# Decoder block in one kernel: the attention loop's links set further apart, with a third score buffer, and the last state-space group's output taken from PSUM

## The reference

```python
scores = jnp.einsum('bsgrd,btgd->bgrst', xq, xk) / math.sqrt(HEAD_DIM) + mask
probs = jax.nn.softmax(scores, axis=-1)
out = jnp.einsum('bgrst,btgd->bsgrd', probs, xv)
x = layernorm(x + mixer(x)); x = layernorm(x + attention(x, ctx, ctx, 0, mask)); x = layernorm(x + ffn(x))
```

## Time and profile before

| | us |
|---|---|
| median of 3 runs | 1813.44 |
| the profiled execution's own time | 1810.98 |
| its span in the trace | 1809.3 |
| PE busy in the span | 1692.5 (94%) |
| DVE busy | 1204.6 (67%) |
| ACT busy | 1107.4 (61%) |
| POOL busy | 710.1 (39%) |

### The profile page before, as it was taken

One profiled execution on the slowest core, in us unless ns is written; L12 is line 12 of the kernel. 1 busy time (PEld: TensorE's weight loads), 2 busy tenths in 40 slices (PEclk: granted clock), 3 DMA queues, 4 the chain that ended last, 5 costly groups with the idle time before them and its releaser, 6 DMA issues.

```text
span 1809.3 us, 26326 instructions
## 1 busy us (share of the span) xinstructions
PE 1692.5 (94%) x9160; PEld 1285.1 (71%) x9160; DVE 1204.6 (67%) x2257; ACT 1107.4 (61%) x2352; POOL 710.1 (39%) x588
## 2 busy tenths in 40 slices
PE   5999999999999999999999999999999867668998
PEld 4777887888788878887788778777877633333556
DVE  4766677767775768577858685868586766555443
ACT  3767485748484949484949484948594545655321
POOL 3354444435452536253626362646263411112000
PEclk8999999999999999999999999999999888889999
DMA  5232222313131323132303131313132800001000
GB/s 192 82 94 90 74 92 84 111 53 106 69 111 54 123 61 115 41 123 82 119 31 122 68 134 41 123 52 124 41 123 69 158 20 1 1 1 36 7 18 24
DMA packets 76551, 138.88 MB, mean 77 GB/s; under 512 B 6786, under 2 KB 13954, under 8 KB 76164
## 3 DMA queue, kind: packets, MB, share of 16 engines
q1 hardware_dynamic: 76420, 137.21, 24.2%
HBM read 134.55 MB, written 2.63 MB: 76 GB/s over the span
## 4 chain that ended last, share of the span: by engine, by line
PE 41%; DVE 34%; ACT 18%; issue 7%; DMA 0%; DVEq 0%; POOL 0%; SPq 0%; ACTq 0%
DVE conv L727 13%; PE ps_hs L1090 6%; ACT ps_dec L528 6%; PE ps_hs L1091 6%; PE ps_hs L1092 6%; DVE xdt L751 4%; DVE m_sb L760 4%; ACT L528 3%; ACT sq_tmp L538 3%; PE ps_y L1314 3%; PE ps_hs L243 3%; DVE ps_y L768 3%; PE ps_hs L245 2%; PE ps_hs L244 2%; PE ps_hs L1275 2%
## 5 line engine op out<-in xcount | busy, mean ns | idle before, releaser
L727 DVE SCALAR_TENSOR_TENSOR conv<-ps_hs,cw,conv 128x508 f32<-128x508 f32 (+2 forms) x432 | 319.2, 739 | 36.8 <-ACT conv L492 26.6
L375 POOL TENSOR_SCALAR_AFFINE_SELECT cum_bc<-cum_bc 128x1024 f32<-128x1024 f32 x128 | 140.4, 1097 | 503.0 <-DMA cum_bc<-cum_scratch 500.9
L528 ACT ACTIVATE ps_dec<-cum_bc,neg_cum 128x128 f32<-128x128 f32 x1024 | 308.7, 356 | 0.8
L760 DVE TENSOR_TENSOR m_sb<-ps_dec,cb 128x512 f32<-128x512 f32 x256 | 169.5, 685 | 154.7 <-ACT ps_dec L528 154.7
L243 PE MATMUL ps_hs<-x_hi,w_hi 128*128 128x512 f32 x576 | 231.8, 402 | 15.8 <-DVE conv L727 8.0
L243 PE MATMUL ps_gate<-x_hi,w_hi 128*128 128x512 f32 x576 | 239.5, 416 | 0.0
L492 ACT ACTIVATE conv<-ps_hs,cbias,cw 128x512 f32<-128x512 f32 x144 | 110.5, 769 | 189.6 <-PE ps_hs L245 189.6
L245 PE MATMUL ps_gate<-x_hi,w_lo 128*128 128x512 f32 x576 | 226.3, 393 | 0.0
L244 PE MATMUL ps_hs<-x_lo,w_hi 128*128 128x512 f32 x576 | 225.4, 391 | 0.0
L245 PE MATMUL ps_hs<-x_hi,w_lo 128*128 128x512 f32 x576 | 225.3, 391 | 0.0
L244 PE MATMUL ps_gate<-x_lo,w_hi 128*128 128x512 f32 x576 | 224.2, 389 | 0.0
(11 more groups left out here) (141 smaller groups left out, 3139.3 us busy)
## 6 DMA issues: line engine op xcount, KB each, us to landing
cum_bc<-cum_scratch SPq DMA_DIRECT2D x128, 512.0 KB, 4.1
w_raw<-w_in SPq DMA_DIRECT2D x145, 256.0 KB, 4.7
wo_raw<-w_out SPq DMA_DIRECT2D x64, 256.0 KB, 5.0
g_acc<-x_t SPq DMA_DIRECT2D x4, 512.0 KB, 5.8
acc<-x_nat SPq DMA_DIRECT2D x1, 2048.0 KB, 9.7
k_rep<-ctx_t SPq DMA_DIRECT2D x8, 256.0 KB, 12.0
out<-y_out SPq DMA_DIRECT2D x8, 256.0 KB, 2.0
wg_sb<-w_gate SPq DMA_DIRECT2D x1, 1792.0 KB, 12.3
```

Of the source, the lines that this page charges most:

```text
L528: x = sc.activation(ps_dec[e][:, cols], cum_bc[bh][:, e, cols], ACT.Exp, bias=neg_cum[:, bh * HB + b, head:head + 1])
L727: v.scalar_tensor_tensor(out=dst, in0=src, scalar=cw[:, at, TAPS - 1 - n:TAPS - n], in1=dst, op0=ALU.mult, op1=ALU.add).then_inc(S["tap"], 1)
L760: v.tensor_tensor(flat(m_sb[:, q]), ps_dec[q % 2][:, :], flat(half(cb, q // 2)), ALU.mult)\
```

## The change

It touches four places; nothing before the last pass of the mixer is changed. What each chunk computes is the same.

1. **Links and buffers of attention.** PE's loop index i now does scores(i+1), values(i-4), turn_probs(i-2); DVE's does keep_turned(i-3), masked(i, 0), masked(i, 1); ACT's does keep_turned(i-3), exponentials(i-1, 0), exponentials(i-1, 1), with keep_values between them and keep_queries ahead of them. `pr`, `pr_t` and `neg_max` get a third buffer.
2. **Values.** The two products of a chunk wait together for both copies.
3. **The mixer's last pass.** `square_sums` goes ahead of the last quarter of the products. DVE adds `g_acc * rstd_g` to `acc` (first_part), and then `ps_hs * rstd_g` straight from the bank (second_part), in place of adding the bank to `g_acc` first.
4. **The drain.** turn_values for the last two halves of sequence 7, its statistics, the second norm's second half and its transposes lie beside hidden tiles 1 to 9, before 0 to 7.

```diff
+X2_STEPS = (27, 29, 31, 33)
-        neg_max = sb3("neg_max", [P, 2, 2 * REP], F32)
+        neg_max = sb3("neg_max", [P, 3, 2 * REP], F32)
-        sb3("fill_w", [P, 2664], F32)
+        pr2 = sb3("pr2", [P, 2 * REP, SEQ], F32)
+        pr_t2 = sb3("pr_t2", [P, 2, HALF], F32)
+        sb3("fill_w", [P, 752], F32)
...
@@ ACT: exponentials and keep_turned use [i % 3] @@
-                need(act, S["pv_ps"], 2 * (i - 2) + 1)
+                need(act, S["pv_ps"], 2 * (i - 3) + 2)
...
-            for i in range(CHUNKS + 2):
-                b, c = i // KD, i % KD
-                if i < CHUNKS:
-                    exponentials(i, 0)
-                if 1 <= i <= CHUNKS:
-                    keep_turned(i - 1)
-                if i < CHUNKS:
-                    exponentials(i, 1)
-                if i >= 3 and i % 2:
-                    keep_values((i - 3) // 2)
-                if c == 3 and b + 1 < BATCH:
-                    keep_queries(b + 1)
-                if i == 4 * HB + 3:
+            for i in range(1, CHUNKS + 3):
+                if 0 <= i - 3 < CHUNKS:
+                    keep_turned(i - 3)
+                if i % KD == 1 and i // KD + 1 < BATCH:
+                    keep_queries(i // KD + 1)
+                if i - 1 < CHUNKS:
+                    exponentials(i - 1, 0)
+                if i % 2 == 0 and i >= 6:
+                    keep_values((i - 6) // 2)
+                if i - 1 < CHUNKS:
+                    exponentials(i - 1, 1)
+                if i == 23:
                     root(2, 0, slice(0, HB))
-                if c == 1 and HB < b < BATCH:
-                    x2_high(b - HB - 1, BACK_PS)
-                if i == CHUNKS - 1:
-                    x2_high(HB - 1, BACK_PS)
+                if i in X2_STEPS:
+                    x2_high(X2_STEPS.index(i), BACK_PS)
...
@@ DVE: the mixer's last pass @@
-            def last_group(b):
-                add_group(GROUPS - 1, b)
-                dve.wait_ge(S["acc_ok"], BATCH * (GROUPS - 1) + b + 1)
-                row_stats(1, b)
+            def second_part(b):
+                dve.wait_ge(S["o_ps"], BATCH * (2 * GROUPS - 1) + b + 1)
+                dve.wait_ge(S["acc_ok"], BATCH * (GROUPS - 1) + b + 1)
+                v.scalar_tensor_tensor(out=acc[:, b, :], in0=ps_hs[b % 2][:, :], scalar=rstd_g[:, b:b + 1],
+                                       in1=acc[:, b, :], op0=ALU.mult, op1=ALU.add).then_inc(S["gacc_ok"], 1)
+                dve.wait_ge(S["gacc_ok"], BATCH * (2 * GROUPS - 1) + b + 1)
+                row_stats(1, b)
...
+            invert_group(GROUPS - 1)
+            first_part(0)
+            first_part(1)
             for b in range(BATCH):
-                v.tensor_tensor(g_acc[:, b, :], g_acc[:, b, :], ps_hs[b % 2][:, :], ALU.add).then_inc(S["gacc_ok"], 1)
...
+                second_part(b)
+                if b + 2 < BATCH:
+                    first_part(b + 2)
                 if b == 4:
+                    variances(1, 0, first_half)
                 if b == 5:
                     inverses(1, 0, first_half)
+                    for n in range(2):
+                        normed(1, n, acc[:, n, :]).then_inc(S["x1_ok"], 1)
...
@@ DVE: attention @@
-            for i in range(CHUNKS + 1):
-                b, c = i // KD, i % KD
+            for i in range(CHUNKS + 3):
+                if i >= 3:
+                    keep_turned(i - 3)
                 if i < CHUNKS:
                     masked(i, 0)
-                if i >= 1:
-                    keep_turned(i - 1)
-                if i < CHUNKS:
                     masked(i, 1)
-                if c == 0 and b >= 1:
-                    attended(b - 1, 0)
...
+                if i % 2 == 0 and i >= 8:
+                    n = (i - 8) // 2
+                    if n % 2:
+                        batch_done(n // 2)
+                    else:
+                        attended(n // 2, 0)
...
+                if (i + 1) % KD == 0 and (i + 1) // KD + 1 < BATCH:
+                    b = (i + 1) // KD + 1
+                    normed(1, b, acc[:, b, :]).then_inc(S["x1_ok"], 1)
+                if i + 2 in X2_STEPS:
+                    b = X2_STEPS.index(i + 2)
+                    normed(2, b, acc[:, b, :]).then_inc(S["x2_ok"], 1)
+                if i in X2_STEPS:
+                    x2_low(X2_STEPS.index(i), BACK_PS)
...
@@ PE: the mixer's last pass @@
                 pe.wait_ge(S["wo_lo_ok"], t + 1)
+                if not more:
+                    pe.wait_ge(S["g_lo_ok"], 2 * t + 1)
+                    square_sums(t)
...
@@ PE: attention @@
-                for par in range(2):
-                    j = 2 * (c % 2) + par
-                    pe.wait_ge(S[("pt_a", "pt_v")[par]], i + 1)
+                pe.wait_ge(S["pt_a"], i + 1)
+                pe.wait_ge(S["pt_v"], i + 1)
+                b = n // 2
+                for j in range(2 * (i % 2), 2 * (i % 2) + 2):
...
-            for i in range(CHUNKS):
-                b, c = i // KD, i % KD
-                scores(i)
-                if c == 0 and b:
-                    turn_values(b - 1, 0)
-                if c == 2 and b:
-                    turn_values(b - 1, 1)
-                if i >= 1:
-                    turn_probs(i - 1)
-                if i >= 2:
-                    values(i - 2)
-                if c == 3 and b + 1 < BATCH:
-                    turn_queries(b + 1)
+            scores(0)
+            for i in range(CHUNKS + 2):
+                if i + 1 < CHUNKS:
+                    scores(i + 1)
+                if i >= 4:
+                    values(i - 4)
+                if i >= 2:
+                    turn_probs(i - 2)
+                if i % 2 and i >= 7:
+                    turn_values((i - 7) // 2)
+                if i % KD == 0 and i // KD + 1 < BATCH:
+                    turn_queries(i // KD + 1)
+                if i + 1 in X2_STEPS:
+                    pe.wait_ge(S["att_ok"], (i - 8) // 2 + 1)
+                    turn_x2(X2_STEPS.index(i + 1), BACK_PS)
...
@@ PE: the drain @@
             hidden(0, 0)
+            values(CHUNKS - 2)
             values(CHUNKS - 1)
             hidden(0, 1)
-            turn_values(BATCH - 1, 1)
+            turn_values(2 * BATCH - 2)
+            hidden(0, 2)
+            turn_values(2 * BATCH - 1)
```

More of the change, by code:

```diff
@@ L674, in _ @@
                     hidden(hf, m)
-                    if hf == 0 and m == 1:
+                    if hf == 0 and m == 0:
+                        keep_values(2 * BATCH - 1)
+                    if hf == 0 and m == 3:
                         root(2, 1, slice(HB, BATCH))
-                    if hf == 0 and HB <= m < 2 * HB:
-                        x2_high(m, ps_gate[m % 2])
+                    if hf == 0 and 6 <= m < 6 + HB:
+                        x2_high(m - 6 + HB, ps_gate[m % 2])
                 for n in range(hf * HB, hf * HB + HB):
@@ L884, in _, with first_part @@
             dve.wait_ge(S["w_lo_ok"], STEPS)
[L885 to L901 removed]
+            def first_part(b):
+                add_group(GROUPS - 1, b)
@@ L982, in _ @@
-                if i == CHUNKS - 2:
-                    normed(2, HB - 1, acc[:, HB - 1, :]).then_inc(S["x2_ok"], 1)
-                if c == 1 and HB < b < BATCH:
-                    x2_low(b - HB - 1, BACK_PS)
-                if i == CHUNKS - 1:
-                    x2_low(HB - 1, BACK_PS)
+                if i % 2 == 0 and i >= 8:
[4 more added lines that the diff above has]
+                        attended(n // 2, 0)
+                    if n == BATCH - 1:
+                        variances(2, 0, first_half)
@@ L1007, in _ @@
                     if m == 0:
+                        attended(BATCH - 1, 0)
+                    if m == 2:
                         batch_done(BATCH - 1)
                         variances(2, 1, second_half)
-                    if m == 2:
+                    if m == 4:
                         inverses(2, 1, second_half)
-                    if m in (2, 3):
-                        for b in range(2 * m, 2 * m + 2):
+                    if m in (4, 5):
+                        for b in range(2 * m - 4, 2 * m - 2):
                             normed(2, b, acc[:, b, :]).then_inc(S["x2_ok"], 1)
-                    if HB <= m < 2 * HB:
-                        x2_low(m, ps_gate[m % 2])
+                    if 6 <= m < 6 + HB:
+                        x2_low(m - 6 + HB, ps_gate[m % 2])
                 for n in range(hf * HB, hf * HB + HB):
@@ L1178, in _ @@
                     out_products(b, TPH - 1).then_inc(S["o_ps"], 1)
-                    if t % TPG == TPG - 1 and b == (BATCH - 1 if more else 1):
+                    if t % TPG == TPG - 1 and more and b == BATCH - 1:
                         square_sums(t)
@@ L1208, in turn_probs @@
                     for r in range(REP):
-                        mm = pe.transpose(ps_gate[par][:, r * SEQ:(r + 1) * SEQ], pr[i % 2][:, par * REP + r, :],
```

(14 more changed lines are left out.)

80 lines of the change are left out of this document (36 added, 44 removed).

## The result

The changed kernel takes 1753.86 us, the median of 4 runs (1751.99 to 1757.1), against 1813.47 before: a ratio of 0.9673 (95% interval 0.9656 to 0.969). The forecast was 1748 with a range of 1737 to 1785. The profiled execution took 1751.99 us, 6.9 more than the 1745.1 that the sum gave for it, and that small difference hides one large miss, on the way in, and smaller ones of the opposite sign.

The account below looks back on a forecast made before the run. The prediction took the chain between in-order engines in attention as the bound. Feed-forward 67.4 us earlier and 1.5 added beside it gave 1745.1 us profiled, 1747.5 with 2.46 to the median, so 1748; range 1737 to 1785.

Parts of the forecast that it names:

- The drain: Beside feed-forward: one more pair of values (0.99) and one more turn_values (0.48) cost PE 1.5 us; ends -1 and +4.
- the sum: Profiled execution: feed-forward starts 67.4 us earlier, 1.5 us is added beside it, so 1810.98 - 65.9 = 1745.1 us.
- the way in: Mixer's last pass to attention: b = 2 at 1440.7, products end 2.0 us later (1457.3), first maximum 2.9 earlier (1459.3).
- What bounds it: Attention, 187.8 us, 5.9 a step: set by the chain between PE, DVE and ACT, none of them full.
- The loop: Attention: two-step loop through ACT's copy, exponentials, keep_values and PE, 7.5 us with hand-overs; 15.0 for four steps, 3.75 a step.
- DVE's floor: Attention, four steps: DVE's own work is 14.3 us with adds of 1.25 us, or 12.8 with adds of 0.42.
- The queries and the clock: Attention: PE's 4.1 us gap before a new sequence goes, and with it what puts the clock down; clock over 0.95.
- the floor's working: Attention, four steps: PE's own work is 13.5 us, of which 5.3 are transposes.
- the third rival: Attention: the clock swings, low for half of the loop, 5.1 us a step, 32 us more: 1780; chance 0.08.
- The table loads and the last steps: Attention: two table loads of 1.28 at step 23, some 2 us stay; steps 27 to 31 take 4.1 us each.
- short stalls: Feed-forward's first half: stalls of PE that might go, given as the lower end, -1 us, of a +1.5 us charge.
- the signs written down: Attention: clock over 0.95, PE over 85% busy, ACT's wait under 25 us, no gap over 2.5, maxima start near 1459.

Follow-up runs that it names:

- values in fours: Changed kernel with the mask's negation moved back to b = 4, and PE doing the values of two chunks together in every odd step: 1732.1 us (0.9579).

## Why the prediction was right, and where it was wrong

**What bounds it: right.** A chain of in-order engines, not an engine. With the distances, and the third buffers that carry them, 5.9 us a step became 3.67. ACT's wait for the maxima went from 75.1 us to nothing.

**The loop: right, and near the mark.** I said 15.0 us for four steps, set by the loop over ACT's copy, four exponentials and `keep_values` and PE's two steps. It is 14.69, its waits are where the loop has them, and taking the copy out of the loop gave 13.9. The four hand-overs of 0.1 us each have no row of their own in any run; a turn of the loop took 7.35 us, which leaves 0.2 for all four beside the 7.1 us of work. The stage from the first maximum to the first feed-forward tile was forecast at 124.3 us and is 122.6.

**DVE's floor: wrong in one term, without effect.** I took 1.18 us for each add into `acc` of `attended`. The median over its 16 adds in the kernel after is 0.425 us (the longest 0.88), for example:

```profile
1527.28 0.42 DVE L943 TENSOR_TENSOR att<-ps_y,rec 128x256 f32<-128x256 f32 x1
1527.74 0.42 DVE L947 TENSOR_TENSOR acc<-acc,att 128x256 f32<-128x256 f32 x1
```

In the kernel before, the ten adds of 1.25 us all begin 0.07 us behind a key block of POOL (1533.43 behind 1533.36), and none of the six shorter ones does. After the change one add of the 16 begins during a key block, and it is the one of 0.88 us. DVE's floor is 12.8, the lower of the two I gave. That the meeting makes the add long fits every add of both traces; no run changed the meeting alone.

**The queries and the clock: half right.** The clock is 1.00 in all of attention in the profiled execution. But shortening the one gap is not enough: with gaps of 2.5 us the mean clock was still 0.87 in the later sequences. In the changed kernel's steady loop the queries' gap is gone and no other is over 0.6 us (PE busy 52.3 of 56 us between 1497 and 1553). Which of its gaps had to go for the clock to stay up, no run shows. By the floor's working 5.3 of 13.5 us of PE's work are transposes, and the clock did not fall, so the third rival did not come true here. The Trainium skill ("TensorE: Matmul & The Clock Gate", Part 4: PE-mode transpose) says that transposes do not count as busy in the same way; in this mix with scores and values they did not bring the clock down.

**The table loads and the last steps: two sizes off, in opposite directions.** Two us of the loads were to stay; 2.7 did (6.66 against 3.97), and behind the gap they leave the clock can fall. Steps 27 to 31 were to take 4.1 each; 27 to 30 took 3.8 in the mean. Step 31 has no scores any more, since they now stand a step ahead; it took 2.4.

**The way in: wrong, the largest miss.** The step said that a bank comes free "after the norm, its inverse, two first parts and a second part" and put b = 2 at 1440.7. It was 1449.2. I had listed what the edit adds on DVE, but not the wait for the mask that it puts ahead of the inverse; the same wait costs nothing at b = 4. First maximum 1470.9 in place of 1459.3, 11.6 us late: 9.4 of that is the wait and what came with it (5.0 us idle, some 2 us of slower instructions on DVE, and half clock on PE's next 12 products), the rest mostly the mixer ending later in that execution (first product at 1432.6 against 1430.8). With the mask moved, b = 2 starts 9.7 us behind the first product; the forecast put it at 9.9. So the parts that the step did count were sized right. Without the wait the new pass brings 2.6 us, the forecast 2.9.

**The drain: wrong in sign.** I charged 1.5 us for two more value products and one more way back. Four products in a row take what two take (1.06 us), so only the way back was to pay, and with the new drain, its root two tiles later, a stall of 1.5 us is gone that I had seen only as "short stalls" in the bound: -1.4 instead of +1.5 (51.9 against 53.3), which is 2.9 us better. Of these, 1.0 is the pair and 1.5 the stall; 0.4 stays open. That the root's place and not another part of the drain removed the stall was not tested by itself.

**Together:** 11.6 us late at the first maximum, 1.7 less in attention (122.6 instead of 124.3), 2.9 less in the drain, so 7.0, where the profiled execution lies 6.9 above the sum. That the total came so near is in part luck: 4.6 us of gains that I had priced too low stand against the miss on the way in. Of the signs written down, the clock, PE's share and ACT's wait came true; the first maximum, the end of the products and the longest gap (3.1 us at the table loads, not 2.5) did not.

**The best versions** of those run have the mask at b = 4 and the values in fours: 1732.1 us, and 1732.35 with `attended` moved as well, which are the same within noise. Between the marks the first is 17.3 us below the changed kernel (9.1 on the way in, 8.2 in attention).

## What to carry to other kernels

When in-order engines hand work round in a ring, list the longest loop through their program orders, not only the sums of their work, and look for a copy that stands behind work nobody is waiting for: moving one 0.5 us copy was worth 6.9 us, more than the two table loads (2.7) and the reordered pass (2.6) together. A distance between links is only as good as the buffers behind it; going back from three buffers to two gave back 50 of 60 us. Of a step that is moved, look up the landing time of every transfer it waits for: a 64 KB mask behind 2.5 MB on its queue cost 9 us, and its row was in the trace of before.

## What the runs showed of the hardware that I had not expected

- Four fp32 products of 128 x 512 into four different quarters of 32 output rows take 1.06 us together, as two do (1.05).
- The clock behind the same gap of PE falls in one kernel's execution and stays in another's. Behind 1.80 us it stayed at 1.00 in the changed kernel and fell in the one without the root; behind 3.1 us it stayed at 1.00 there and fell in the one with the mask moved. Where it falls, it can do so late: behind a 2.45 us gap that ended at 1540.17 the scores still ran at full clock, and the transposes at 1542.70 at half. With gaps of 0.6 us at most it stayed at 1.00 over 56 us of the changed kernel, 39% of PE's work there being transposes.
- An add of 128 x 256 on VectorE that begins just behind a key block of POOL took 1.25 us in the kernel before, in ten cases of ten, and 0.42 apart from them. The negation of the mask took 1.00 us beside POOL's copy in the changed kernel and 0.22 in the kernel before.
- The four executions of the changed kernel differ by 5 us and order by their mean clock: 1752.0 at 0.989, 1753.0 at 0.988, 1754.8 at 0.987, 1757.1 at 0.985.
